# Self-attention scores in four 32-row pieces, one burst for 512 tokens, and turned probabilities in borrowed banks

## What is computed

```python
x = x + _L0_attn_ref(_layernorm(x, axis=-1), L0_attn_w_q, L0_attn_w_k, L0_attn_w_v, L0_attn_w_o)
# with HEADS = 32, D_K = 16:
q, k, v = (proj(w_q), proj(w_k), proj(w_v))
scores = jnp.einsum('bhqd,bhkd->bhqk', q, k) / jnp.sqrt(jnp.float32(D_K))
attn = jax.nn.softmax(scores, axis=-1)
out = jnp.einsum('bhqk,bhkd->bhqd', attn, v)
out = out.transpose(0, 2, 1, 3).reshape(B, S, HIDDEN)
return jnp.einsum('bse,oe->bso', out, w_o)
```

## Time and profile before

| | |
|---|---|
| median of 3 runs | 1543.92 us (1543.82 to 1548.12) |
| profiled execution | 1547.11 us, span of its instructions 1545.3 us |
| TensorE matmuls | 1466.8 us busy, 95% of the span |
| VectorE | 1111.0 us, 72% |
| ScalarE | 420.5 us, 27% |
| GpSimd | 484.0 us, 31% |
| mean granted TensorE clock | 0.98 of full speed |

### The profile page before, as it was taken

How to read it: one execution, slowest core, us unless ns; L and a number is a source line. 1 busy time by engine, 2 the same in 40 slices (tenths; PEclk the granted TensorE clock), 3 DMA queues, 4 the chain that set the end, 5 groups by cost and what they waited for, 6 DMA issues and landing times.

```text
span 1545.3 us, 25394 instructions
## 1 busy us (share of the span) xinstructions
PE 1466.8 (95%) x10080; PEld 1173.3 (76%) x10080; DVE 1111.0 (72%) x1664; ACT 420.5 (27%) x726; POOL 484.0 (31%) x427
## 2 busy tenths in 40 slices
PE   6999999999997579999999999999999999998998
PEld 5788887777775467878777877878877778786776
DVE  3555553687788777788787787787887878888653
ACT  4111233445543221221221221222222212221321
POOL 4322210333332223423423433333323324323022
PEclk9999999999999789999999999999999999999999
DMA  8465320000000410110010010021020110003011
GB/s 249 134 207 174 108 71 0 2 21 15 9 2 1 150 55 15 41 56 26 31 55 28 28 58 31 22 69 28 15 69 28 29 54 28 28 15 107 1 48 62
DMA packets 79108, 83.93 MB, mean 54 GB/s; under 512 B 9824, under 2 KB 50928, under 8 KB 78736
## 3 DMA queue, kind: packets, MB, share of 16 engines
q1 hardware_dynamic: 68976, 63.42, 13.0%
q10 hardware_dynamic: 9216, 16.78, 3.3%
q0 software_dynamic: 800, 2.11, 0.6%
HBM read 59.22 MB, written 23.07 MB: 53 GB/s over the span
## 4 chain that ended last, share of the span: by engine, by line
PE 62%; DVE 2%; issue 1%; POOL 1%; DMA 0%; ACT 0%; POOLq 0%; SPq 0%; DVEq 0%; ACTq 0%
PE p_ps_q L75 9%; PE p_ps_y L1084 8%; PE p_ps_y L1085 8%; PE p_ps_y L1086 8%; PE p_ps_q L76 8%; PE p_ps_q L77 8%; PE p_ps_s L1046 4%; PE p_ps_o L1071 4%; PE p_ps_p L1056 2%; PE p_ps_y L1666 1%; PE p_ps_y L1668 1%; PE p_ps_y L1667 1%; PE p_ps_q L1629 1%; PE p_ps_o L156 1%; PE p_ps_q L1638 0%
## 5 line engine op out<-in xcount | busy, mean ns | idle before, releaser
L1392 POOL TENSOR_TENSOR p_q_rot<-p_ra,p_rb 128x512 f32<-128x512 f32 x128 | 166.9, 1304 | 286.7 <-DVE p_rb L164 286.7
L1084 PE MATMUL p_ps_y<-p_wo_hi,p_o_hi 128*128 128x512 f32 x512 | 212.3, 415 | 2.2 <-DVE p_o_lo L1279 2.0
L75 PE MATMUL p_ps_q<-p_xt_hi,p_wq_hi 128*128 128x512 f32 x512 | 211.7, 413 | 0.0
L76 PE MATMUL p_ps_q<-p_xt_lo,p_wq_hi 128*128 128x512 f32 x512 | 202.7, 396 | 0.0
L1085 PE MATMUL p_ps_y<-p_wo_lo,p_o_hi 128*128 128x512 f32 x512 | 202.7, 396 | 0.0
L1086 PE MATMUL p_ps_y<-p_wo_hi,p_o_lo 128*128 128x512 f32 x512 | 202.4, 395 | 0.0
L77 PE MATMUL p_ps_q<-p_xt_hi,p_wq_lo 128*128 128x512 f32 x512 | 201.4, 393 | 0.0
L1384 POOL TENSOR_TENSOR p_pn<-p_p,p_inv 128x512 f32<-128x512 f32 x64 | 66.9, 1045 | 301.3 <-DVE p_inv L1259 301.3
L1180 ACT ACTIVATE p_o_hi<-p_ps_o 128x512 fp32r<-128x512 f32 x128 | 69.5, 595 | 282.0 <-PE p_ps_o L1071 279.6
L1289 DVE TENSOR_TENSOR x_sb<-p_ps_y,x_sb 128x512 f32<-128x512 f32 x128 | 88.0, 687 | 78.6 <-PE p_ps_y L1086 78.6
L162 DVE TENSOR_TENSOR p_ra<-p_ps_q,p_cos_t 128x512 f32<-128x512 f32 x128 | 85.9, 671 | 59.9 <-PE p_ps_q L77 56.5
(11 more groups left out here) (224 smaller groups left out, 3025.7 us busy)
## 6 DMA issues: line engine op xcount, KB each, us to landing
p_raw_q<-in_wq SPq DMA_DIRECT2D x36, 256.0 KB, 3.8
v_scratch<-p_v_out SPq DMA_DIRECT2D x32, 256.0 KB, 2.7
k_scratch<-p_k_out SPq DMA_DIRECT2D x32, 256.0 KB, 2.1
p_k_t<-k_scratch ACTq DMA_DIRECT2D x32, 256.0 KB, 2.6
p_v_in<-v_scratch ACTq DMA_DIRECT2D x32, 256.0 KB, 2.8
p_raw_o<-in_wo SPq DMA_DIRECT2D x32, 256.0 KB, 3.8
x_sb<-in_x SPq DMA_DIRECT2D x16, 256.0 KB, 2.8
out<-p_yb SPq DMA_DIRECT2D x16, 256.0 KB, 2.0
```

The source lines that it names most:

```text
L75: nc.tensor.matmul(out, lh, rh, start=(c == 0), stop=False)
L76: nc.tensor.matmul(out, lh, rl, start=False, stop=False)
L1084: nc.tensor.matmul(ps_y[t][:, :], oh, w_hi["o"][h][:, :], start=(h == 0), stop=False)
L1392: nc.gpsimd.tensor_tensor(q_rot[:, h, :], ra[:, :], rb[:, :], ALU.add).then_inc(q_added, 1)
```

## The change

An iteration is no longer cut into two units. Scores are taken for the whole iteration at once, in four pieces of 32 partitions (two heads each) over four banks of ps_s: 32 fp32 matmuls with 128 stationary columns (q_x) and 64 moving ones (k_x, which is now a plain copy of k: `copy_k` takes the place of `spread_k`, with one activation instead of two). For this the columns of wq and wk are permuted outside the kernel. Shift, exponentials and inversion go by halves of two banks, of the same size as a unit was. ps_p is gone: the four pieces of turned probabilities go to ps_qk, ps_o and the first two banks of ps_s. p and pt lie over wv_hi and wv_lo, so the exponentials wait for the last value product. move_values moves to ScalarE. TensorE's order in a pass `it` is scores(it), project k(it + 1), output 0 and 1 of it - 2, turn(it - 1), project q(it + 1), output 2 and 3 of it - 2, mix(it - 1). In the value stage scores(0) is one burst, the second projection of k comes before it, and the shifts of iteration 0 come at tiles 14 and 15.

```diff
@@ -476,11 +476,10 @@
         SCALE = 1.0 / float(np.sqrt(np.float32(D1)))
         ITS = G1 * NB
         BB = BLOCK // SEQ
-        UNITS, UB = 2, BB // 2
-        PARTS, PB = 4, BB // 4
-        UNITS_ALL, PARTS_ALL = ITS * UNITS, ITS * PARTS
-        ROWS, SPAN = 2, P // 2
-        COLS, PCOLS = ROWS * UB * SETS, ROWS * PB * SETS
+        ROWS, SPAN = 4, P // 4
+        HALF_ROWS, HALVES = ROWS // 2, 2
+        PARTS, PB = 4, BB // 2
+        COLS = ROWS * BB
...
-        k_x = [m.sb(f"k_x{i}", [P, BB, SETS, SEQ]) for i in range(2)]
+        k_x = [m.sb(f"k_x{i}", [P, BLOCK]) for i in range(2)]
         v_x = [m.sb(f"v_x{i}", [P, BB, HPG1 // 2, 2 * D1]) for i in range(2)]
-        s, p = m.sb("s", [P, COLS, SEQ]), m.sb("p", [P, COLS, SEQ])
-        pn = [m.sb(f"pn{i}", [P, PCOLS, SEQ]) for i in range(2)]
-        pt = [m.sb(f"pt{i}", [P, ROWS * PB, P]) for i in range(2)]
+        s = m.sb("s", [P, ROWS, BB * SEQ])
+        pn = m.sb("pn", [P, HALVES * BB, 2, SEQ])
+        spare = m.sb("spare", [P, 1024])
...
+        p = nc.alloc_sbuf_tensor_at("p3_p", [P, ROWS, BB * SEQ], F32, offset=base + 154 * 1024)
+        pt = nc.alloc_sbuf_tensor_at("p3_pt", [P, HALVES * BB, P], F32, offset=base + 162 * 1024)
...
-        ps_p = [m.ps(f"ps_p{i}") for i in range(2)]
-        ps_s = m.ps("ps_s", (P, ROWS, UB * SETS * SEQ))
+        ps_s = m.ps("ps_s", (P, ROWS, BB * SEQ))
         ps_y = m.ps("ps_y", (P, 2, HIDDEN))
-        ps_t, ps_v = [ps_y[:, i, :] for i in range(2)], [ps_o, ps_p[0]]
+        ps_t, ps_v = [ps_y[:, i, :] for i in range(2)], [ps_o, ps_qk]
+        ps_p = [ps_qk, ps_o, ps_s[:, 0, :], ps_s[:, 1, :]]
...
         def projection_bank(w, it):
 
-            return ps_p[1] if w == "k" and it < 2 else ps_qk
+            return ps_s[:, 2 * it + "qk".index(w), :] if it < 2 else ps_qk
...
-                if it < 2:
-                    need(pe, {"q": q_spread, "k": k_spread}[w], it)
-                elif w == "k":
+                if it > 1 and w == "k":
                     need(pe, q_spread, it)
-                else:
-                    need(pe, k_spread, it + 1)
+                    need(pe, v_copied, TILES)
+                elif it > 1:
+                    need(pe, pt_copied, (it - 2) * PARTS + 1)
...
+            def scores(it):
+
+                need(pe, q_spread, max(it + 1, 2))
+                need(pe, k_spread, max(it + 1, 2))
+                need(pe, s_shifted, it * HALVES)
+                need(pe, pt_copied, (it - 1) * PARTS)
+                for b in range(BB):
                     for r in range(ROWS):
                         rows = slice(r * SPAN, (r + 1) * SPAN)
-                        mm = nc.tensor.matmul(ps_s[:, r, b * SETS * SEQ:(b + 1) * SETS * SEQ],
-                                              q_x[it % 2][rows, first + b, :, :].rearrange("p e q -> p (e q)"),
-                                              k_x[it % 2][rows, first + b, :, :].rearrange("p m k -> p (m k)"), start=True, stop=True)
+                        mm = nc.tensor.matmul(ps_s[:, r, b * SEQ:(b + 1) * SEQ], q_x[it % 2][rows, b, :, :].rearrange("p e q -> p (e q)"),
+                                              k_x[it % 2][rows, b * SEQ:(b + 1) * SEQ], start=True, stop=True)
                 mm.then_inc(s_done, 1)
...
+            def turn(it):
+
+                for u in range(PARTS):
+                    need(pe, p_norm, it * PARTS + u + 1)
+                    if u == 0:
+                        need(pe, k_spread, min(it + 3, ITS))
+                    elif u == 1:
+                        need(pe, out_lo, it)
+                    else:
+                        need(pe, s_shifted, min((it + 1) * HALVES + 1, ITS * HALVES))
+                    for i in range(PB):
+                        tr = nc.tensor.transpose(ps_p[u][:, i * P:(i + 1) * P], pn[:, u * PB + i, :, :].rearrange("p j k -> p (j k)"),
+                                                 ident[:, :])
+                    tr.then_inc(p_turned, 1)
+
+            def mix(it):
+
+                need(pe, pt_copied, (it + 1) * PARTS)
+                need(pe, v_placed, it + 1)
+                need(pe, v_moved, it + 1)
+                need(pe, out_lo, it)
+                for b in range(BB):
                     for c in range(HPG1 // 2):
-                        r, e = c // SETS, c % SETS
+                        h, e = c // SETS, c % SETS
                         mm = nc.tensor.matmul(ps_o[c * 2 * D1:(c + 1) * 2 * D1, b * SEQ:(b + 1) * SEQ], v_x[it % 2][:, b, c, :],
-                                              pt[j % 2][:, r * PB + i, e * SEQ:(e + 1) * SEQ], start=True, stop=True)
+                                              pt[:, h * BB + b, e * SEQ:(e + 1) * SEQ], start=True, stop=True)
...
                 if t == 11:
+                    project("k", 1)
+                if t == 12:
                     scores(0)
-                if t == 12:
-                    project("k", 1)
-                if t == 13:
-                    scores(1)
...
+            for it in range(1, ITS + 2):
+                if it < ITS:
+                    scores(it)
+                if it + 1 < ITS:
+                    project("k", it + 1)
+                if it > 1:
+                    output(it - 2, 0)
+                    output(it - 2, 1)
+                if it <= ITS:
+                    turn(it - 1)
+                if it + 1 < ITS:
+                    project("q", it + 1)
+                if it > 1:
+                    output(it - 2, 2)
+                    output(it - 2, 3)
+                if it <= ITS:
+                    mix(it - 1)
...
+            def copy_k(it):
                 need(act, done["k"], it + 1)
-                need(act, s_done, (it - 1) * UNITS)
-                for j in range(SETS):
...
+                need(act, s_done, it - 1)
+                nc.scalar.activation(k_x[it % 2][:, :], projection_bank("k", it)[:, :], ACT.Copy).then_inc(k_spread, 1)
+
+            def exponentials(it, h):
+                need(act, s_shifted, it * HALVES + h + 1)
+                need(act, p_norm, (it - 1) * PARTS + (h + 1) * HALVES)
+                need(act, v_done, TILES)
+                rows = slice(h * HALF_ROWS, (h + 1) * HALF_ROWS)
+                nc.scalar.activation(p[:, rows, :], s[:, rows, :], ACT.Exp, scale=SCALE).then_inc(p_exp, 1)
+
+            def copy_turned(it, u):
+                need(act, p_turned, it * PARTS + u + 1)
+                need(act, pv_done, it)
+                nc.scalar.activation(pt[:, u * PB:(u + 1) * PB, :].rearrange("p i q -> p (i q)"), ps_p[u][:, :], ACT.Copy).then_inc(pt_copied, 1)
+
+            def move_values(it):
+
+                need(act, pv_done, it - 1)
+                need(act, zeroed, 2)
+                need(act, v_copied, min((it + 1) * TPB, TILES))
+                for r in range(2):
+                    dst, src = value_parts(it, r, 1 - r)
+                    c = nc.scalar.activation(dst, src, ACT.Copy)
+                c.then_inc(v_moved, 1)
 
...
-                if t == 9:
+                if t == 7:
+                    move_values(0)
+                if t == 10:
                     act.wait_ge(heads_in, 16)
                     spread_q(0)
+                    copy_k(0)
                 if t == 11:
-                    spread_k(0)
+                    spread_q(1)
                 if t == 12:
-                    spread_q(1)
-                if t == 14:
-                    exponentials(0)
-                    spread_k(1)
+                    copy_k(1)
             copy_values(TILES - 1)
...
+            exponentials(0, 0)
+            exponentials(0, 1)
+            for it in range(1, ITS + 2):
                 g, b = group_of(it), block_of(it)
...
+                if it > 1:
+                    outputs_hi(it - 2)
+                if b == 2 and 0 < g < G1:
+                    split_hi(act, "o", g, y_done, (it - 2) * TPB)
+                if it < ITS:
+                    move_values(it)
+                if it + 1 < ITS:
+                    copy_k(it + 1)
+                if it < ITS:
+                    exponentials(it, 0)
+                if it <= ITS:
+                    for u in range(3):
+                        copy_turned(it - 1, u)
+                if it < ITS:
+                    exponentials(it, 1)
+                if it <= ITS:
+                    copy_turned(it - 1, 3)
+                if b == NB - 2 and g + 1 < G1:
+                    split_hi(act, "k", g + 1, done["k"], it + 2)
+                if it + 1 < ITS:
+                    spread_q(it + 1)
+                if b == NB - 2 and g + 1 < G1:
                     split_hi(act, "q", g + 1, done["q"], it + 2)
...
+            def half(tensor, h):
+                return tensor[:, h * HALF_ROWS:(h + 1) * HALF_ROWS, :].rearrange("p r (b k) -> p (r b) k", k=SEQ)
+
+            def shift(it, h):
...
+                nc.vector.tensor_reduce(mx[:, cols], half(ps_s, h), AX.X, ALU.max).then_inc(s_max, 1)
```

(142 more changed lines are left out.)

74 lines of the change are left out of this document (17 added, 57 removed).

## The result

The changed kernel takes 1523.62 us (median of 4 runs, 1522.29 to 1524.21) against 1543.87 (4 runs, 1543.80 to 1548.12): a ratio of 0.9861, 95% interval 0.9843 to 0.9879, 20 us faster. The forecast was 1524.

> The changed kernel as it is, beside the next three on one chip, as their base. Theory: the same ratio to the kernel before as measured (0.986), waits of TensorE of 3.0 us at the stage's start and 9.2 at its end, passes of 13.17 us.

A forecast was written before the change was run, and what follows sets the result against it. TensorE was taken to bound the self-attention stage, with VectorE 8% behind in the last group. Terms -12.5 - 7.8 + 1.3 + 0.6 - 1.3 = -19.7 us, say -20, gave 1524 us; range 1508 to 1536.

The forecast's parts named there:

- (1): TensorE's order in the self-attention stage: 76 fewer changes of array shape at 0.165 us each, -12.5 us.
- (2): Scores in sets of four 32-row pieces: the weight side keeps the step at 0.11 us, no gain.
- rival B: Scores: the moving side sets the pace, 0.83 us less per iteration, 1513 us; chance 0.20.
- rival C: Scores: four loads share what two share, a set takes 0.22 us, 1548 us, slower than before; chance 0.12.
- (3): TensorE's waits for wq_lo and q_x at the three changes of the group of heads go, -7.8 us.
- (4): Steady pass: no new TensorE waits, smallest slack 0.5 us; 0, with up to 0.5 us for each of the last three passes.
- rival D: Steady pass: waits replace the shape changes' cost, a pass runs 0.5 us late at turn or scores, 1532 us; chance 0.13.
- (5): Start of the self-attention stage: exponentials wait for the last value product, TensorE's waits grow, +1.3 us.
- (6): End of the self-attention stage: pipeline an iteration deeper, TensorE waits 12.0 us against 11.4 before, +0.6 us.
- (7): Value stage: one score burst instead of two and no wait for xt_lo, -1.3 us.
- (8): Granted clock: half-clock stretches after the start and end waits stay the same, 0, with 3 us either way.

The follow-up runs named there:

- E1: Changed kernel with mix cut into two halves and one output tile between them, two more shape changes in each of 15 passes; 1532.20 us.
- E5: Changed kernel with only one of the two heads in each score piece (32 x 64 pieces, four side by side, every second head left out); 1512.59 us.
- E6: Changed kernel with 32 moving columns instead of 64 in each score piece, second half of the keys left out; one execution, passes of 13.14 us.
- E2: Changed kernel with scores in 64-row pieces of 128 moving columns as before, with two masked copies of k; 1530.10 us.
- E7: Changed kernel with one tiny exponential on ScalarE at tile 14 of the value stage, so the activation table loads there; 1521.85 us.
- E4: Changed kernel with each 32 x 128 score piece cut into two of 32 x 64, eight side by side, same scores; 1519.74 us.
- E8: Changed kernel with another VectorE order in the last three passes: an addition between the shifts, statistics behind additions and outputs_lo; 1517.33 us.

## Why the prediction was right

The total was right to 0.4 us. Its parts, by the steps of the prediction, were less exact.

(1) Changes of shape: the mechanism is shown by E1, at 0.15 us each, which makes 76 x 0.15 = 11.4 against 12.5. Two units of before exceed a pass by 0.87 us for five changes, so 0.174 each, and 76 x 0.174 = 13.2. What a change into 32-row pieces costs was unknown; by this average it isn't dearer than the others.

(2) The scores: no gain, since the step stays at 0.111. The reading from the load times was right, and E5 and E6 show the stationary columns as the cause: rival B (the moving side sets the pace) and rival C (four loads share what two share) are both out. Four loads of 128 columns stream in the time of two: 186 ns each, and four records every 0.111 us. The Trainium skill ("TensorE: Matmul & The Clock Gate", "LDWEIGHTS (loading the stationary operand)") says that the time goes by columns and not by rows; the 32 x 128 loads of after take 186 ns, the 64 x 128 ones took 187. What the prediction cites from the Trainium skill's "What overlaps and what doesn't" is said there of a load beside running matmuls of other row groups, not of loads beside each other; for those the evidence is this trace.

(3) Group changes: 7.8 forecast. A group exceeds two plain units by 2.25 us in the traces, so 3 x 2.25 + 0.3 = 7.0. The term that was too large is the 0.16 us that I added to each wait. A change of shape lies in the same gap as each of these waits and would hide in it; no run tests that reading.

(4) No new wait in the steady pass: right, and rival D is out. The least slack (turn's first piece, 0.5) was real: E2 puts 0.65 us on ScalarE in front of it, and 0.24 of wait appear. ScalarE's copy of 64x256 takes 0.415 us where I took 0.4. The remark that VectorE is on a par with TensorE in the last group holds for one of its four passes. The additions lie two passes behind, so the statistics come that much later. VectorE in pass 12, the group's first, and in pass 15, its last (columns as in the earlier trace rows):

```profile
408.23:421.40 13.17, 13.17 (x187) 11.20 (x181) 10.61 (x12) 7.36 (x12) 4.84 (x7) 1.00 0.01 3
447.73:460.90 13.17, 9.70 (x163) 7.67 (x156) 12.96 (x16) 5.98 (x10) 4.80 (x7) 0.87 0.01 2
```

E5's passes 12 to 14 are 12.31 like those before.

(5) The start: waits of 3.0 us against 2.6 before, +0.5 where I had +1.3; the table load was bare as forecast (E7).

(6) The end: 12.0 us forecast, 9.2 shown, 10.1 before; -0.9 instead of +0.6. The largest wait was to be 4.8; the longest seen is the 2.9 for o_lo.

(7) The value stage: -1.7 (forecast -1.3).

(8) The clock: TensorE was busy for 11.5 us at half clock in the stage before and for 11.4 after (11.3 in the rows below, whose windows are cut to tenths), so zero was right in sum. Not in place: the start has no such stretch any more, and the end has three instead of one. The start's share in that is partly luck, as E1 has a stretch there behind waits that are no longer. Stretches of after:

```profile
455.90:459.30 3.40, 3.30 (x26) 2.29 (x30) 3.37 (x5) 0.43 (x1) 0.58 (x1) 0.50 0.00 0
462.70:466.10 3.40, 3.11 (x8) 2.42 (x9) 0.38 (x2) 0.00 (x0) 0.06 (x1) 0.50 0.00 0
473.00:479.80 6.80, 4.88 (x11) 2.81 (x9) 2.99 (x4) 0.00 (x0) 0.00 (x0) 0.50 0.00 0
```

By the traces the value and the self-attention stage changed by 1.7 + 20.6 = 22.3 us, against 19.7 in the sum. The parts account for it: 13.2 in (1), 7.0 in (3), -0.5 in (5), 0.9 in (6) and 1.7 in (7) make 22.3. The forecast was low by 0.7 in (1), 0.8 in (5), 1.5 in (6) and 0.4 in (7), and high by 0.8 in (3). The medians of the runs differ by only 20.3; the traces are of one execution of each kernel, and which of the two figures is nearer the worth of the change stays open. So the mechanisms were right, and the agreement to 0.4 us is partly luck.

## What to carry to other kernels

Group the stages of a TensorE program by the shape into which they split the array: a change costs 0.15 to 0.17 us here even with a full queue, and transposes between wide products cost none. Splitting a small contraction over more row groups halved the moving columns here and left the step as it was, since the stationary ones were the more numerous; cutting those did (0.43 us a pass in E4, with all the work kept). At the end of a pipelined stage order the engine that holds TensorE by who waits for it (6.3 us in E8): a wait can count once for itself and again for the clock.

## What the runs showed of the hardware that I had not expected

Eight 32 x 64 pieces side by side reach a step of 0.058 us at first; behind the first 32 records it is 0.091, 11.4 ns per record, where four pieces (E5) hold 0.058, 14.6 ns per record, to the end. Moving columns cut from 64 to 32 leave the step as it is at 128 stationary ones (a pass of 13.14 us instead of 13.17). The granted clock fell at the start of the stage in E1, for 3.4 us, and not in the changed kernel, whose waits there are no shorter.
